# Attention scores computed twice with the keys on the partitions

## The reference

```python
    x = x + jnp.tanh(g_xattn[0]) * _L0_xattn_ref(_layernorm(x, axis=-1), ctx_4096, ctx_4096, ...)
    x = x + jnp.tanh(g_ffn[0]) * _L0_ffn_ref(_layernorm(x, axis=-1), ...)
# inside _L0_xattn_ref, after projections with a mixing of the four parts:
        scores = jnp.einsum('bhqdm,bhkdm->bhqkm', qh, kh) / math.sqrt(dk)
        weights = jax.nn.softmax(scores, axis=3)
        out = jnp.einsum('bhqkm,bhkdm->bhqdm', weights, vh)
        return out @ Wo.T + bo
```

## Time and profile before

| | |
|---|---|
| median of three runs | 1499.09 us (1498.79 to 1502.88) |
| profiled execution | 1503.86 us |
| its span, first to last instruction | 1502.1 us |
| mean granted TensorE clock | 0.982 |
| TensorE busy over the span | 95% |
| VectorE, ScalarE, GpSimd busy | 50%, 38%, 21% |
| attention stage | from 622.77 to 1101.72 us |

### The profile page before, as it was taken

The page is one execution under the profiler, slowest core; times in us unless marked ns, Lnnn a source line. Parts: engine busy times, 40 slices in busy tenths (PEclk is TensorE's granted clock), DMA queues, the critical chain, the costliest instruction groups (busy, mean ns, idle before and its releaser), DMA issues. The chain is left out here.

```text
span 1502.1 us, 24552 instructions
## 1 busy us (share of the span) xinstructions
PE 1432.6 (95%) x8976; PEld 1187.2 (79%) x8976; DVE 747.9 (50%) x1628; ACT 574.8 (38%) x2432; POOL 316.9 (21%) x304
## 2 busy tenths in 40 slices
PE   7999999999999999389999999999968999999998
PEld 6887887878888888268888888888756888888887
DVE  5322121222555552398888888888857325333210
ACT  3211101111222222399988888888614011110100
POOL 0000000000000000178766666666500000000000
PEclk9999999999999999699999999999979999999999
DMA  5653444434545555777878778678451211211101
GB/s 192 194 176 128 147 159 125 156 127 141 194 148 174 181 169 178 204 222 200 196 187 202 175 182 209 171 183 206 136 224 43 84 71 57 85 43 70 57 28 56
DMA packets 162359, 220.81 MB, mean 147 GB/s; under 512 B 11968, under 2 KB 110272, under 8 KB 160192
## 3 DMA queue, kind: packets, MB, share of 16 engines
q1 hardware_dynamic: 162240, 219.25, 49.2%
HBM read 135.32 MB, written 83.89 MB: 146 GB/s over the span
## 5 line engine op out<-in xcount | busy, mean ns | idle before, releaser
L852 ACT ACTIVATE prob<-bank,negmax 128x128 f32<-128x128 f32 x1024 | 361.4, 411 | 52.7 <-DVE negmax L885 49.9
L921 POOL TENSOR_TENSOR prob<-prob,rec 128x512 f32<-128x512 f32 x256 | 266.4, 1042 | 140.8 <-DVE rec L893 140.6
L852 ACT ACTIVATION_READ_ACCUMULATOR prob<-bank,negmax 128x1 f32 x1024 | 236.1, 249 | 0.0
L885 DVE TENSOR_REDUCE negmax<-bank 128x4 f32<-128x512 f32 x256 | 176.4, 690 | 72.5 <-PE bank L799 70.0
L899 DVE COPY probT<-bank 128x512 f32<-128x512 f32 x256 | 169.8, 663 | 1.3 <-PE bank L808 0.9
L494 DVE SCALAR_TENSOR_TENSOR stage_lo<-bank,bias_mixed,stage_hi 128x512 fp32r<-128x512 f32 x64 | 48.1, 751 | 241.2 <-ACT stage_hi L496 241.2
L148 PE MATMUL bank<-place_a,w_hi 128*128 128x512 f32 x384 | 151.4, 394 | 6.8 <-DVE place_a L141 6.8
L808 PE MATMUL bank<-ident,prob 128*128 128x128 f32 x1024 | 155.4, 274 | 0.0
L150 PE MATMUL bank<-place_a,w_lo 128*128 128x512 f32 x384 | 149.6, 390 | 0.0
L149 PE MATMUL bank<-place_a,w_hi 128*128 128x512 f32 x384 | 149.5, 389 | 0.0
L496 ACT ACTIVATE stage_hi<-bank,bias_mixed 128x512 fp32r<-128x512 f32 x64 | 44.1, 689 | 266.0 <-PE bank L150 243.3
(11 more groups left out here) (163 smaller groups left out, 2565.9 us busy)
## 6 DMA issues: line engine op xcount, KB each, us to landing
k_in<-k_stack SPq DMA_DIRECT2D x192, 96.0 KB, 3.9
k_stack<-stage_hi SPq DMA_DIRECT2D x64, 256.0 KB
v_pad<-v_out SPq DMA_DIRECT2D x32, 512.0 KB, 2.7
q_stack<-stage_hi SPq DMA_DIRECT2D x64, 256.0 KB
v_place<-v_pad SPq DMA_DIRECT2D x16, 1024.0 KB, 8.7
v_place<-x_mid SPq DMA_DIRECT2D x30, 512.0 KB, 3.8
first_q<-q_stack SPq DMA_DIRECT2D x64, 192.0 KB, 4.5
q_in<-q_stack SPq DMA_DIRECT2D x64, 192.0 KB, 3.7
```

The lines of the kernel that those rows point to most:

```text
L852: last = act.activation(prob[t % NP][:, j, :], sc_bank[t % NSC][:, j * P:(j + 1) * P], ACT.Exp, bias=negmax[:, t % NS, j:j + 1], accum_out ...
L885: dve.tensor_reduce(negmax[:, t % NS, :], sc_bank[t % NSC][:].rearrange("p (j k) -> p j k", j=4), AX.X, ALU.max, negate=True).then_inc(s_m ...
L921: pool.tensor_tensor(prob[t % NP][:], prob[t % NP][:], rec[:, t % NS, :].unsqueeze(2).to_broadcast([P, 4, P]), ALU.mult).then_inc(s_norm, 1)
```

## The change

Keys and queries are stored in another layout: per batch and octet, two sets of rows of 4 x 128 columns, with 48 rows of data each. In the keys' tile there are two more rows, of ones. In the queries' tile, in the same two rows, stand zeros at first, and later the high and the low part of the negated maximum. So 98 rows are multiplied.

Scores are computed with the keys as the stationary operand, so that keys are on the partitions and queries in the columns: four matmuls of 256 columns per octet. This is done twice. After the first time VectorE takes the maximum over the keys, with a reduction that transposes 32x32 blocks on the way, one more transpose and two minima; GpSimd splits it in two parts, and SP places these as the two rows of the queries' tile with two DMAs of 4 KB (`place_max`). Three slots later TensorE computes the scores again, now with the maximum subtracted, and ScalarE takes two exponentials of 512 columns each. They come out with the keys on the partitions, as the product with the values wants them, so no transposes and copies are needed.

The values' tile has ones in its unused columns, so that the product with the values also gives the sums. It is done once per half, for four octets together, into two banks. ScalarE brings four masked copies out of PSUM, GpSimd merges them in pairs, VectorE transposes the sums, inverts them and spreads the inverses by another transpose, and GpSimd multiplies. The result is split by ScalarE and GpSimd, projected by TensorE, gated by ScalarE, and added to the residual by GpSimd. The ring of keys and queries has six places, and a load waits for the second scores of the octet six back.

In the first stage each store of a projection is cut in two, in pieces of 128 columns; three DMAs write the rows of ones and zeros (1.5 MB together); and the order of columns in `mix` and the values is another.

```diff
-    k_stack = nc.dram_tensor("k_stack", (HM, 3, DK, T), F32, kind="Internal").ap()
-    q_stack = nc.dram_tensor("q_stack", (HM, 3, DK, T), F32, kind="Internal").ap()
+    k_rows = nc.dram_tensor("k_rows", (NB, NOCT, 2, KROWS, 4 * P), F32, kind="Internal").ap()
+    q_rows = nc.dram_tensor("q_rows", (NB, NOCT, 2, QROWS, 4 * P), F32, kind="Internal").ap()
...
-        KQ = 4
+        first_q = sb("first_q", [ROWS, 2, 4, P], F32R)
+        first_k, second_k = (sb(n, [ROWS, 4, P], F32R) for n in ("first_k", "second_k"))
+        KQ = 6
...
         def load_kq(sp, o, k_tile, q_tile, landed):
 
-            b, first = o // NOCT, (o % NOCT) * OCT
-            tok = slice(b * P, (b + 1) * P)
-            sp.dma_start(
-                q_tile[:].bitcast(F32),
-                q_stack[first:first + OCT, :, :, tok].rearrange("(p a) s d t -> (a s d) p t", a=2)
-            ).then_inc(landed, 16)
-            for a in range(2):
-                sp.dma_start(
-                    k_tile[a * STACK:(a + 1) * STACK, :, a, :].bitcast(F32),
-                    k_stack[first + a:first + OCT:2, :, :, tok].rearrange("p s d t -> (s d) p t")
-                ).then_inc(landed, 16)
+            b, c = o // NOCT, o % NOCT
+            k_flat = k_rows[b, c].rearrange("a r f -> (a r) f")
+            q_flat = q_rows[b, c].rearrange("a r f -> (a r) f")
+            sp.dma_start(k_tile[:].rearrange("r p t -> r (p t)").bitcast(F32), k_flat[0:ROWS, :]).then_inc(landed, 16)
+            sp.dma_start(q_tile[0:KROWS, 0].rearrange("r p t -> r (p t)").bitcast(F32),
+                         q_flat[0:KROWS, :]).then_inc(landed, 16)
+            sp.dma_start(q_tile[STACK:ROWS, 1].rearrange("r p t -> r (p t)").bitcast(F32),
+                         q_flat[KROWS:2 * KROWS, :]).then_inc(landed, 16)
...
-                        sp.dma_start(scratch[c * OCT:(c + 1) * OCT, section, :, g * GT:(g + 1) * GT],
-                                     src[:].bitcast(F32)).then_inc(s_stage[slot], 16)
+                        for a in range(2):
+                            sp.dma_start(
+                                scratch[g * GB:(g + 1) * GB, c, a, section * DK:(section + 1) * DK, :].rearrange(
+                                    "b d (p t) -> (d p) b t", t=P),
+                                src[a * 64:(a + 1) * 64, :].rearrange("f (b t) -> f b t", t=P).bitcast(F32)
+                            ).then_inc(s_stage[slot], 16)
...
 
                 def empty(bank):
-                    def by_pair(ap):
-                        return ap.rearrange("p (q a d) -> p q a d", a=2, d=DK)
+                    def by_head(ap):
+                        return ap.rearrange("t (c a d p) -> t c p a d", a=2, d=DK, p=4)
...
+                        def store_rows(sp):
+                            zeros, ones = (v[:].rearrange("p q a d -> p (q a d)") for v in v_out)
+                            q_all = q_rows.rearrange("b c a r f -> (b c) (a r f)")
+                            k_all = k_rows.rearrange("b c a r f -> (b c) (a r f)")
+                            width, at = 4 * P, STACK
+                            sp.wait_ge(s_even, 2)
+                            for i in range(2):
+                                sp.dma_start(q_all[:, (at + 2 * i) * width:(at + 2 * i + 2) * width], zeros).then_inc(s_rows, 16)
+                            sp.dma_start(k_all[:, at * width:(at + 2) * width], ones).then_inc(s_rows, 16)
+                        plan.append((len(line.jobs) + 0.65, store_rows))
                     if (g, c) == (NG - 1, 1):
 
                         def zero_first(dve):
                             line.wait_filled(dve, t_end[2 * NB - 1])
...
+            NPT = 5
+            probT = [sb(f"probT{i}", [P, 2, 2, 2, P], F32, st) for i in range(NPT)]
+            NS = 3
+            part = [sb(f"part{i}", [P, 2, 4, 4], F32, st) for i in range(NS)]
+            turned = sb("turned", [P, 32], F32, st)
+            pairs_min = sb("pairs_min", [P // 2, 32], F32, st)
...
+            LAG = 3
+            FIRST_V, O_LAG = 4 + LAG, 9
+            SLOTS = FIRST_V + 4 * (HALVES - 1) + O_LAG + 8
+
+            def half_at(s, lag):
+
+                h, rest = divmod(s - FIRST_V - lag, 4)
+                return h if rest == 0 and 0 <= h < HALVES else None
+
+            def proj_at(s):
+
+                h, j = divmod(s - FIRST_V - O_LAG, 4)
+                if not 0 <= h < HALVES or j == 3:
+                    return []
+                return [(h, i // 4, i % 4) for i in ((0, 1, 2, 3, 4, 5, 6, 7)[8 * j // 3:8 * (j + 1) // 3])]
...
+                def place_max(o):
+                    row = q_in[o % KQ]
+                    for i, (tile, ready) in enumerate(((neg_hi, s_nhi), (neg_lo, s_nlo))):
+                        sp.wait_ge(ready, o + 1)
+                        sp.dma_start(row[STACK + i:STACK + i + 1].rearrange("r a p (b t) -> r (a p b) t", t=32).bitcast(F32),
+                                     tile[o % NS][:].bitcast(F32)).then_inc(s_neg[o % KQ], 16)
...
+                for s in range(SLOTS):
+                    if 1 <= s <= OCTS:
+                        place_max(s - 1)
+                    if s + LAG < OCTS:
+                        load_oct(s + LAG)
...
+                    if h is not None:
+                        if h % 2 and h // 2 + 2 < NB:
+                            load_v(h // 2 + 2)
+                        if h % 2:
+                            load_xb(h // 2)
...
+                for s in range(SLOTS):
+                    work = proj_at(s)
+                    if s < OCTS:
+                        slot = s % KQ
+                        pe.wait_ge(s_kq[slot], 48 * (s // KQ + 1))
+                        for p in range(4):
+                            if s and p % 2 == 0:
+                                pe.wait_ge(s_part, 2 * s - 1 + p // 2)
+                            dst = one_bank[p // 2][:].rearrange("k (a p q) -> k a p q", a=2, p=2)[:, :, p % 2, :]
+                            last = pe.matmul(dst, k_in[slot][:, p, :], q_in[slot][:, :, p, :], start=True, stop=True,
+                                             skip_group_check=True)
+                            if p % 2:
+                                last.then_inc(s_one, 1)
...
+                        pe.wait_ge(s_exp, 8 * h + 8)
...
+                        if h:
+                            pe.wait_ge(s_ev, 4 * h)
+                        for i in range(4):
+                            o = 4 * h + i
+                            for a in range(2):
+                                for p in range(4):
+                                    last = pe.matmul(
+                                        v_bank[a][32 * p:32 * p + 32, i * P:(i + 1) * P],
+                                        v_in[b % 2][:, 4 * (o % NOCT) + p, a, :], probT[o % NPT][:, p // 2, a, p % 2, :],
+                                        start=True, stop=True, skip_group_check=True)
                         last.then_inc(s_pv, 1)
...
+                    for part_of in work[:(len(work) + 1) // 2]:
+                        project(*part_of)
+                    o = s - LAG
+                    if 0 <= o < OCTS:
+                        slot = o % KQ
+                        pe.wait_ge(s_neg[slot], 32 * (o // KQ + 1))
+                        for p in range(4):
+                            if o and p % 2 == 0:
+                                pe.wait_ge(s_exp, 2 * o - 1 + p // 2)
+                            dst = two_bank[p // 2][:].rearrange("k (a p q) -> k a p q", a=2, p=2)[:, :, p % 2, :]
+                            last = pe.matmul(dst, k_in[slot][:, p, :], q_in[slot][:, :, p, :], start=True, stop=True,
+                                             skip_group_check=True)
+                            if p % 2:
+                                last.then_inc(s_two, 1)
+                    for part_of in work[(len(work) + 1) // 2:]:
+                        project(*part_of)
 
...
+                for s in range(SLOTS):
+                    o = s - LAG
+                    if 0 <= o < OCTS:
+                        if o >= NPT:
+                            act.wait_ge(s_pv, (o - NPT) // 4 + 1)
+                        for i in range(2):
+                            act.wait_ge(s_two, 2 * o + i + 1)
+                            act.activation(probT[o % NPT][:, i].rearrange("k a p q -> k (a p q)"), two_bank[i][:],
+                                           ACT.Exp).then_inc(s_exp, 1)
...
+                        act.activation(raw_o[:], v_bank[0][:], ACT.Copy, scale=side[:, 0:1]).then_inc(s_ev, 1)
+                        act.activation(other[:], v_bank[1][:], ACT.Copy, scale=side[:, 1:2]).then_inc(s_ev, 1)
...
+                        act.activation(raw_s[:], v_bank[0][:], ACT.Copy, scale=side[:, 1:2]).then_inc(s_ev, 1)
+                        act.activation(sums_t[:], v_bank[1][:], ACT.Copy, scale=side[:, 0:1]).then_inc(s_ev, 1)
...
+                for s in range(SLOTS):
+                    if s < OCTS:
```

(28 more changed lines are left out.)

397 lines of the change are left out of this document (186 added, 211 removed).

## The result

The changed kernel took 1528.32 us (median of four runs, 1517.65 to 1535.44) against 1499.24 beside it: ratio 1.018, 95% interval 1.012 to 1.025. It is slower, by 29 us; the forecast was 52 us faster. The profiled execution took 1528.27 (span 1525.4, 23.3 more than before).

What follows compares the result with a forecast made beforehand. TensorE's own list was taken to bound the attention stage. From 1503.86 us profiled, -78 (attention), +29 (late loads) and -3 (first stage) made -52: 1452, or 1447 for the median; range 1412 to 1505.

Steps and rivals of the forecast that it cites:

- the sync queue: Loads and placements in attention: loads behind each 1.5 MB land late, 1.8 us per batch, +29 us, bounds 0 and 56.
- the 3.3: Sign of a wrong forecast: a slot of steady attention over 3.3 us, where 2.85 was expected.
- TensorE's list: Attention stage: scores, projections and weighted sum take 11.4 us per four octets, 2.85 per octet against 3.53 before.
- VectorE: Attention stage: its work takes 2.4 us an octet, with 0.60 per transposing maximum, hidden with 0.4 to spare.
- The rival's 1552: VectorE becomes the bound if the transposing maximum costs 1.2 us: 3.9 us per octet, 1552 us in all; chance 0.14.
- ScalarE and GpSimd: Attention stage: ScalarE takes 2.2 us and GpSimd 2.35 us per octet, both hidden below TensorE's 2.85.
- The fear of slots with two large GpSimd operations: Attention slots with two large GpSimd operations (2.56 + 0.4 us) have no room; the next negated maximum waits behind them.
- First stage: Projection stores in more, smaller pieces plus 1.5 MB of constant rows: -3 us, bounds -6 and +6.
- Ends of the stage: Attention stage's start and end: 20 us for the first six slots, 25 us at the end.
- its 430: Whole attention stage with late loads: 430 us against 478.9 before, a gain of 49; 401 without lateness.
- the loads become the bound: Rival: every octet's load lands late and a slot goes to about 3.4 us; +70 instead of +29, 1487; chance 0.18.
- The round trip: Rival: the maximum's way back takes longer than three slots if every landing takes 6.5 us; slot 3.7, 1527; chance 0.13.

Runs made afterwards that it cites:

- e8: Changed kernel with the 1.5 MB burst in six pieces in six slots, and GpSimd's two bias additions moved to emptier slots; 1471.6 us, ratio 0.980.
- e1: Changed kernel with the batch's 1.5 MB of values and residual rows issued in six 256 KB pieces, each in its own slot; 1479.6 us, ratio 0.986.
- e7: Changed kernel with its burst, without the placements of the maximum rows and the waits for them; 1509.7 us, ratio 1.006.
- e16: Changed kernel with values in two halves in other slots than the residual rows, bias additions moved, gated copies and GpSimd's first addition a slot earlier; 1475.1 us, ratio 0.982.
- e4: Changed kernel with both large loads of each batch, whole, issued into ScalarE's queue at the same place; 1530.1 us, ratio 1.018.
- e5: Changed kernel with 14 extra 512-column matmuls ahead of the second scores once in eight slots, where TensorE stood idle; 1518.1 us, ratio 1.012.

## Why the prediction was wrong

Its bottleneck and its list were right, and the step that failed is the one on the sync queue: "I price 1.8 us per batch, 16 x 1.8 = +29 us; bounds 0 and 56." A slot took 3.64 us, above the 3.3 that the forecast itself had named as the sign that it is wrong.

- *TensorE's list*, 11.4 us per four octets: 11.50 in most of the steps without a long wait, 11.64 in the one shown. Scores, weighted sum and projections each came as priced.
- *VectorE*: the transposing maximum took 0.687 us and 0.60 was taken; the 32-column transpose 0.21. Right, and never the bound, but for the first minimum, below. The rival's 1552 rests on 0.7 us an octet for the work of a half, where the list above it has 0.43; with 0.43 a maximum of 1.2 us gives some 1518.
- *ScalarE and GpSimd*: 0.60 for an exponential, 1.27 to 1.29 for a large GpSimd operation, as priced. The fear of slots with two large GpSimd operations was right in kind, 8 us (e8), but most of it came by the gated copy and not by the maximum that was named.
- *First stage*: -3 was taken, -4.5 came.
- *Ends of the stage*: 47.6 us were taken for what lies outside the 31 steps (401 - 31 x 11.4); 28.0 and 27.4 came, 7.8 more.
- *The sync queue*: 31 steps cost 451.1 us, 97.7 over the list, against 29. That is 69 of the 76 us by which the stage missed its 430. Two things were wrong in it. The burst was priced at the best rate in the trace, 295 GB/s, as if it had the engines to itself, and its lateness as what exceeds one load's slack. It took 9.1 us from its second issue (814.78 to 823.92), with the octets' loads moved beside it, and the placement behind it took 8.6, one that TensorE needed before it needed the load. And nothing was allowed for the clock. The waits in the rows add up to 60 us; a tenth of the clock missing over 391 us of busy TensorE is some 39 more (an estimate), and together they come close to the 97.7. Even the upper bound, 56, left that out.
- *Rivals*: "the loads become the bound" came nearest to the cause, but spread over all slots; e1 shows that the same bytes, evenly issued, fit. Whether loads of 98 and 50 rows land later for their row counts, as it also held, no run separates. "The round trip" gave 1527, close to the measured time, for a reason that e7 shows to be at most 19 us of it: a time that agrees proves no mechanism. It needed a landing of 6.5 us "for every octet"; 36 of 128 took over 6.
- Without its lateness the forecast would have been 1418, and e8 took 1471.6: 31 steps of 12.68 instead of 11.4 are 40 us of it, and the ends 8. TensorE's waits from 640 to 1073 us add up to 26 of the 40 (8.6 for loads, 7.9 for the gated copy, 6.3 for placements, the rest shorter), and some 10 are the clock (an estimate): it was 0.85 from 646 to 700 us in e8, and 0.83 in the changed kernel, where the kernel before had 0.99 from 640 to 700. That the attention stage starts at a lower clock was in no term of the sum. The forecast had treated engines with 0.4 us to spare a slot as costing nothing. Which of these is the last to go is not settled; e16 shows that taking one away lets the next come up.

## What to carry to other kernels

When a new small transfer must make a round trip within a few slots, look at what is issued beside it, and price its landing as that of the whole burst together with the loads that stand around it in the queue, not as the burst alone at the peak rate. Spread large prefetches that have many slots to land over those slots; that cost a few lines here and decided the sign of the change. And price each wait of TensorE of some microseconds twice, once for itself and once for the half clock behind it (here 3.2 and some 2 us).

## What the runs showed of the hardware

- Moving a burst to another engine's queue did not let small transfers pass it: of 128 placements of 4 KB, 34 took over 6 us to land in e4 and 36 in the changed kernel, and TensorE's longest wait changed its name (48.3 us for the queries' load).
- The granted clock fell to 0.50 behind 3.16 us of idle time and was back at 1.00 after some 7 us of work without a gap (825.69 to 833); 3.3 us of matmuls in the gap kept it at 1.00 (e5).
- VectorE's first minimum, 64x32 and both inputs in SBUF, takes 0.19 us alone, and 1.36 in this case while GpSimd works on SBUF. In e1, VectorE and then GpSimd:

```profile
858.36 0.21 DVE L966 STREAM_TRANSPOSE turned<-part 128x32 f32<-128x32 f32 x1
858.61 1.36 DVE L967 TENSOR_TENSOR pairs_min<-turned 64x32 f32<-64x32 f32 x1
860.00 0.18 DVE L970 TENSOR_TENSOR negmax<-pairs_min 32x32 f32<-32x32 f32 x1
```

```profile
857.40 1.27 POOL L1024 TENSOR_TENSOR o_norm<-raw_o,other 128x512 f32<-128x512 f32 x1
858.64 1.28 POOL L1001 TENSOR_TENSOR xb<-xb,gated 128x512 f32<-128x512 f32 x1
860.25 0.20 POOL L1016 CAST neg_hi<-negmax 32x32 fp32r<-32x32 f32 x1 [0.33 <-DVE negmax L970]
```

  It ends when GpSimd's addition does (859.97 and 859.92); the transpose ahead of it, with one input, keeps its 0.21 beside GpSimd's work. The mean is 0.29 us in the changed kernel and 0.43 in e1, and every such delay lies on the maximum's round trip. The Trainium skill (SBUF — State Buffer, section on the two separate sides) says that a VectorE operation with two SBUF inputs and a GpSimd operation that reads SBUF hold the shared port pair in turn, each for its whole length. The trace agrees, 1.36 against 0.19; the forecast had used 0.19. What it costs in time alone was not measured.
